# Two small loads on another queue, an early table load, another instruction for the candidate update, and a mask over the whole width

## The reference

```
adj  = s * cond * softmax(x) / sqrt(512)        # 512 x 512 per sequence, diagonal set to -inf
mask = 1 where adj is among the 5120 largest of its sequence, else 0
x    = x + mask
```

## Time and profile before

| | |
|---|---|
| median of three runs | 1718.7 us |
| the profiled execution | 1722.43 us, of which span 1720.7 us |
| PE busy | 1621.3 us (94%) |
| DVE busy | 1181.7 us (69%) |
| ACT busy | 863.5 us (50%) |
| POOL busy | 142.3 us (8%) |
| mean granted PE clock | 0.998 |

### The profile page before, as it was taken

One profiled execution on the slowest core, in us unless ns is written; L12 is line 12 of the kernel. 1 busy time (PEld: TensorE's weight loads), 2 busy tenths in 40 slices (PEclk: granted clock), 3 DMA queues, 4 the chain that ended last, 5 costly groups with the idle time before them and its releaser, 6 DMA issues.

```text
span 1720.7 us, 22533 instructions
## 1 busy us (share of the span) xinstructions
PE 1621.3 (94%) x8268; PEld 1356.1 (79%) x8268; DVE 1181.7 (69%) x2548; ACT 863.5 (50%) x1630; POOL 142.3 (8%) x81
## 2 busy tenths in 40 slices
PE   0759999999899999999999999999999999999998
PEld 0757888888777888888878888888878888888887
DVE  6776877767885887776775787776676576665321
ACT  3546566655753555554571555554472455444240
POOL 4002312213340000000000000000000000000000
PEclk9999999999999999999999999999999999999999
DMA  7023434437566332134454332323344431332453
GB/s 300 1 104 114 165 125 178 155 109 281 195 247 231 117 123 100 72 123 147 147 195 175 150 123 76 121 105 140 137 181 181 161 123 50 122 123 75 171 196 122
DMA packets 62702, 247.94 MB, mean 144 GB/s; under 512 B 4224, under 2 KB 4352, under 8 KB 60672
## 3 DMA queue, kind: packets, MB, share of 16 engines
q1 hardware_dynamic: 62592, 246.50, 38.7%
HBM read 191.95 MB, written 54.53 MB: 143 GB/s over the span
## 4 chain that ended last, share of the span: by engine, by line
PE 81%; DVE 12%; ACT 3%; issue 1%; DVEq 1%; DMA 0%; SPq 0%; ACTq 0%
PE bank L1053 23%; PE bank L1055 23%; PE bank L1054 23%; PE bank L1147 7%; DVE tb L738 3%; DVE cand L795 1%; DVE act L932 1%; DVE prob L908 1%; PE bank L1215 1%; PE bank L1210 1%; PE bank L1173 1%; PE bank L1077 1%; ACT prob L619 1%; PE bank L1211 1%; PE bank L1095 1%
## 5 line engine op out<-in xcount | busy, mean ns | idle before, releaser
L1053 PE MATMUL bank<-xT,w 128*128 128x512 f32 x704 | 279.8, 397 | 0.5 <-POOL w L468 0.5
L619 ACT ACTIVATE prob<-bank,nbias 128x512 f32<-128x512 f32 x256 | 176.6, 690 | 202.2 <-DVE nbias L905 202.2
L1055 PE MATMUL bank<-xT,w 128*128 128x512 f32 x704 | 274.2, 389 | 0.0
L1054 PE MATMUL bank<-xT,w 128*128 128x512 f32 x704 | 274.1, 389 | 0.0
L1053 PE MATMUL bank<-act,w 128*128 128x512 f32 (+1 forms) x576 | 218.2, 379 | 0.8 <-DVE act L869 0.8
L1055 PE MATMUL bank<-act,w 128*128 128x512 f32 (+1 forms) x576 | 211.6, 367 | 0.0
L1054 PE MATMUL bank<-act,w 128*128 128x512 f32 (+1 forms) x576 | 211.5, 367 | 0.0
L916 DVE TENSOR_TENSOR probT<-bank,probT 128x512 fp32r<-128x512 f32 x256 | 158.8, 681 | 24.8 <-ACT probT L629 24.5
L899 DVE TENSOR_REDUCE rowmax<-bank 128x1 f32<-128x512 f32 x256 | 174.6, 682 | 0.0
L1055 PEld LDWEIGHTS bank<-xT,w 128*128 128x128 f32 x704 | 132.2, 188 | 27.7
L1053 PEld LDWEIGHTS bank<-xT,w 128*128 128x128 f32 x704 | 132.1, 188 | 25.9 <-POOL w L468 0.9
(11 more groups left out here) (131 smaller groups left out, 3040.6 us busy)
## 6 DMA issues: line engine op xcount, KB each, us to landing
w<-split_weights SPq DMA_DIRECT2D x144, 1024.0 KB, 5.3
split_weights<-w SPq DMA_DIRECT2D x48, 1024.0 KB, 6.1
wraw<-weights_in SPq DMA_DIRECT2D x48, 512.0 KB, 3.9
adaw<-ada_w_in SPq DMA_DIRECT2D x4, 1536.0 KB, 14.7
xr<-x_in SPq DMA_DIRECT2D x4, 1024.0 KB, 7.4
out<-x SPq DMA_DIRECT2D x4, 1024.0 KB, 4.4
adj<-x_in SPq DMA_DIRECT2D x3, 1024.0 KB, 6.9
adj<-x_in SPq DMA_DIRECT2D x4, 256.0 KB, 4.4
```

Source lines behind the costliest of these rows:

```text
L619: nc.scalar.activation(prob[:, i, :], bank[i][:, :], ACT.Exp, bias=nbias[:, i:i + 1], scale=SCALE, accum_out=rowsum[:, i:i + 1]).then_inc( ...
L1053: pe.matmul(dst, w_hi_ap, x_hi_ap, start=first, stop=False)
L1054: pe.matmul(dst, w_hi_ap, x_lo_ap, start=False, stop=False)
L1055: return pe.matmul(dst, w_lo_ap, x_hi_ap, start=False, stop=last)
```

## The change

Four things are edited.

1. The loads of `small` and `tb` leave SP's queue and are issued by ACT, as its first two instructions, `small` first.
2. ACT then waits for the constants and computes an exponential of a constant column into the spare tile `table`; its wait for `small_in` moves behind `topk_exp(0)`.
3. The move of `cand` is a `tensor_scalar` whose only tensor input is `cand`, with `step_up` as a scalar per partition, in place of a `scalar_tensor_tensor` of the two tiles.
4. The mask's two operations run once over all 2048 elements instead of once per tile; `xm_ready` is raised once a sequence; the statistics come behind, by `row_stats`, four instructions in a row.

```diff
             def first_sequence():
                 load_raw(2, EARLY)
-                wait_apart(sp, xm_ready, NT)
+                wait_apart(sp, xm_ready, 1)
...
-                    wait_apart(sp, xm_ready, (b + 1) * NT)
+                    wait_apart(sp, xm_ready, b + 1)
...
-            sp.dma_start(tb[:, :], cond[0:1, :].to_broadcast([P, T])).then_inc(tb_in, 16)
-            sp.dma_start(small[:, :], cols).then_inc(small_in, 16)
             load_raw(0, 2)
...
+            act_e.dma_start(small[:, :], cols).then_inc(small_in, 16)
+            act_e.dma_start(tb[:, :], cond[0:1, :].to_broadcast([P, T])).then_inc(tb_in, 16)
+            act_e.wait_ge(consts_ready, 3)
+            nc.scalar.activation(table[:, :], ident[:, 0:1], ACT.Exp)
+            topk_exp(0)
             act_e.wait_ge(small_in, 16)
-            act_e.wait_ge(consts_ready, 3)
-            topk_exp(0)
...
-                move = V.scalar_tensor_tensor(cand[:, :], step_up[:, :], -bit / 2, cand[:, :], ALU.add, ALU.add)
+                move = V.tensor_scalar(cand[:, :], cand[:, :], step_up[:, :], -bit / 2, ALU.add, ALU.add)
...
-                for i in range(NT):
-                    part = slice(i * T, (i + 1) * T)
-                    V.scalar_tensor_tensor(eqm[:, part], rank[:, part], need[:, :], low[:, part],
-                                           ALU.subtract, ALU.is_le)
-                    dve.drain()
-                    V.tensor_tensor(xm[:, i, :], xr[:, i, :], eqm[:, part], ALU.add).then_inc(xm_ready, 1)
-                    dve.drain()
-                    V.bn_stats(stats[:, i, 0, :], xm[:, i, :])
+                V.scalar_tensor_tensor(eqm[:, :], rank, need[:, :], low[:, :], ALU.subtract, ALU.is_le)
+                dve.drain()
+                V.tensor_tensor(xm[:, :, :].rearrange("p i d -> p (i d)"),
+                                xr[:, :, :].rearrange("p i d -> p (i d)"), eqm[:, :], ALU.add)\
+                    .then_inc(xm_ready, 1)
+                dve.drain()
...
                             topk_mask(b + 1)
+                            row_stats(xm, 0, 0, D)
                             normalise(b * LNS + LNS, xm, 1)
...
             topk_mask(0)
+            row_stats(xm, 0, 0, D)
             normalise(0, xm, 1)
```

## The result

The changed kernel takes 1707.9 us (1706.7 to 1709.1, six runs) against 1719.2 us (1718.3 to 1722.4, six runs) for the kernel before: ratio 0.9926, 95% interval 0.9916 to 0.9937. The medians lie 11.3 us apart, and the interval stands for 10.8 to 14.4 us. The forecast was 1703.9 against 1718.7, 14.8 us faster, with a range of 1699.5 to 1711. Run again later beside the kernel before, it took 1707.1 against 1720.7, 13.6 us: ratio 0.9920 (0.9906 to 0.9934), which stands for 11.4 to 16.2 us.

The account below looks back on a forecast made before the run. PE, busy 94% of the span, bounds the kernel; gains lie in its gaps at the start and in sequence 0. 2.85 + 5.8 - 1.4 + 1.45 + 6.3 - 0.2 = 14.8 us off 1718.7 gives 1703.9, range 1699.5 to 1711.

Parts of the forecast that it names:

- Edits 1 and 2: At the start, exponentials no longer wait for small; line 761 starts at 8.65 instead of 11.49, gaining 2.85 us.
- the price of sharing: At the start, small and tb move beside the tiles of x and delay them 0.6 us, 1.2 at most.
- rival (c): At the start, ACT's queue is served last, so small and tb land late: 1725.3 us, chance 4%.
- The stall of 5.8 us at the start: Between 21 and 39 us, candidate updates wait for POOL's subtractions; the one-tensor form removes 5.79 us.
- The scalar per partition: In the new candidate update, reading step_up this way costs 0.043 us each, 1.4 us lost over 32 updates.
- Rival (b): The new candidate update stalls beside POOL as the old one did: 1711.5 us, chance 6%.
- Edit 4 at the start: The first mask, run over the full width, takes 7.5 us instead of 8.98 to the statistics' aggregation: 1.45 us won.
- Sequence 0: Faster updates and next mask during this sequence save 1.8 + 2.9 + 1.6 = 6.3 us, bounds 0 and 9.9.
- The wait of 2.93: PE's longest wait, at 526.93 us for the gate behind the mask, goes whole: 2.9 us won.
- The clock: Behind PE's longest wait, 3.4 us at granted clock 0.54 return to full clock: 1.6 us won.
- rival (a): The end of sequence 0 gives nothing, since wide mask operations delay POOL's weight splits: 1710.2 us, chance 20%.
- the same difference: The 14.8 us taken off the profiled 1722.43 us was also taken off the median 1718.7, giving 1703.9 us.

Follow-up runs that it names:

- e2: The kernel before with only the candidate update changed to a tensor_scalar with one tensor input: 1715.0 us, ratio 0.9959 to before.
- e3: The kernel before with only the mask changed, run over the whole 2048 width instead of tile by tile: 1714.3 us, ratio 0.9956 to before.
- f1: The changed kernel with the candidate update a scalar_tensor_tensor again, but step_up in PSUM: 1702.9 us, ratio 0.9899 to before.
- g1: The changed kernel with cand two equal columns wide and the update covering both: 1715.9 us, ratio 0.9972 to before.

## Why the prediction was right, and where its sizes were off

**Edits 1 and 2: the mechanism right, the price of sharing too small.** I took 0.6 us for the slip of the tiles and named 1.2 as the most; the last maximum slipped 1.55 (7.82 to 9.37), and the gain to the first reciprocal was 2.13 us, not 2.85, outside my 2.2 to 3.45. What failed is the bound, which took the extra bytes alone. Not every tile slipped: the first landed as before, the last two 1.55 us later, though `small` and `tb` had landed by 5.70 us. Why that is more than their bytes is not shown. The pair is also not the whole record. In the four profiles with the old loads (before twice, e2, e3) the first reciprocal starts at 10.42 to 11.49 us, since `small` lands anywhere from 8.85 to 9.91; in the seven with `small` and `tb` first on ACT's queue it starts at 9.00 to 9.66. The means are 1.7 us apart, and the 11.49 that I subtracted from is the latest of its four.

Both queues were served at once (the rows of q1 and q10 above), and `small` landed after 1.8 us with SP's queue full, so rival (c), a second queue served last, is refuted. The trace agrees with the Trainium skill (DMA: Bandwidth & Descriptors, Queues, rings and completion order), which has each engine go round between queues.

**Edit 3: right, and its condition shown.** The stall of 5.8 us at the start went whole. The scalar per partition costs 0.214 - 0.159 = 0.055 us an update, 1.76 us for 32, where I took 0.043 and 1.4; f1 took it away and got 1.5 us back. Rival (b) is refuted for one element per partition and confirmed for two (g1). The rule of the Trainium skill (Vector Engine (DVE) Microarchitecture Reference, §5.1) holds for the one even width run; where it counts a matching odd size in, the measurement of a width of one decides against it for that width, and no run has an odd width above one. The sentence of the prediction that names line 905 as bearing the rule out for wide tiles is a slip: its own paragraph (b) has line 908 for that, and line 905, one element wide, speaks against it.

**Edit 4 at the start: right**, 1.62 us for 1.45; the four statistics took 2.48 us for 2.64. The start as a whole gave 7.70 us, where the parts of the sum for it come to 8.7, and most of what is missing is the price of sharing.

**Sequence 0: right, nearly in its parts too.** 6.96 us for 6.3. The wait of 2.93 went whole, as in e3 and not in e2. The aggregation came 11.2 us behind the mask's start, for which the working gave 11.3 (4.1 us earlier than before, 3.9 forecast). The waits for counts fell from 5.0 to 3.5 us, 1.5 for 1.8. The clock gave the 1.7 for which I had 1.6. Some 0.8 us of PE's busy time that went as well is not explained. PE's only wait for POOL's subtraction in that stretch is 0.5 us, as before, so rival (a) did not occur. The later sequences cost 0.4 us together, for 0.2.

**From the profile to the median: the step that failed.** I subtracted 14.8 us from the median by the same difference. The profile pair bears the sum out (14.3), but the changed kernel's profile lies 0.3 us above its median of 1707.9, where that of before lies 3.2 above its 1719.2. That one had two stretches at half clock, worth about 1.7 us each, and the latest start of its kind; the 1.6 us I claimed for the second stretch is a gain only over executions that have it. The changed kernel has such stretches as well, elsewhere and not each time. In the two sessions in which both kernels ran the medians differ by 11.3 and 13.6 us. No execution of before near 1718.4 us was profiled; the granted clocks on record say that the shorter ones have less half clock, not which stretch is missing.

## What to carry to other kernels

Where GpSimd and VectorE work at once, count for each tiny VectorE operation the tensors it reads from SBUF: a second one, or a width of two in a one-input form, can cost it up to 2.2 us beside a GpSimd subtraction of 2.3, while with one of two tensors in PSUM, or one input of width one, no update was held. Before a number is carried from a profiled execution to a median, see how far they are apart and which waits of the one the other may lack. Look also at how late a start that hangs on a load is in other profiles of the same code. A small load that something waits for deserves its own queue, but a large one beside it makes the loads that are needed first land later.

## What the runs showed of the hardware that I had not expected

- An operation with two tensors, one of them in PSUM and one in SBUF, was not held by GpSimd: 157 to 160 ns in 128 times, of which nine began during a GpSimd subtraction, where the form with both in SBUF took up to 2219 ns.
- A `tensor_scalar` of 128x2 with a scalar per partition took up to 2183 ns beside GpSimd, the same of 128x1 at most 218.
- Each of the 16 stretches of 3.4 us at 1.2 GHz in twelve profiles (the one at the very end left out) begins close to the end of a wait of PE of 1.7 us or more, from 0.2 us before it to 1.6 us behind it. It came with all 5 of the waits of 2.3 to 3.1 us ahead of line 1173, with 8 of the 12 of 2.0 to 2.4 us near 140 to 150 us, with 3 of the 12 of 1.71 to 1.73 us for a count in the later sequences, and with none of the 12 of 1.66 us at that place. So the same wait of the same kernel can be followed by half clock in one execution and not in the next; whether its length decides is not shown.
